# Moving the two layer-norm steps on GpSimd past the rotary products

## The reference

```python
x = L0_attn_x
x = x + attention(layernorm(x), qkv_w, proj_w, proj_b, slopes)
x = x + linear(layernorm(x), W, b, V_r, C)
# attention: q, k turned by rotary angles; softmax(q k^T * SCALE + alibi) v; projection
# linear:    x @ W.T + b + (x @ V_r) @ C.T
```

## Time and profile before

| | |
|---|---|
| median of 3 runs | 2132.45 us (2125.33 to 2133.05) |
| the profiled execution | 2133.05 us, of it span 2131.4 us |
| busy, share of the span | PE 98%, PEld 56%, DVE 89%, ACT 71%, POOL 61% |
| mean granted TensorE clock | 0.981 of full |
| one batch, 16 slots, in the steady part | 62.93 us |

### The profile page before, as it was taken

One profiled execution on the slowest core, in us unless ns is written; L12 is line 12 of the kernel. 1 busy time (PEld: TensorE's weight loads), 2 busy tenths in 40 slices (PEclk: granted clock), 3 DMA queues, 4 the chain that ended last, 5 costly groups with the idle time before them and its releaser, 6 DMA issues.

```text
span 2131.4 us, 81879 instructions
## 1 busy us (share of the span) xinstructions
PE 2080.3 (98%) x33572; PEld 1197.8 (56%) x33572; DVE 1894.1 (89%) x5439; ACT 1514.1 (71%) x2562; POOL 1301.3 (61%) x1095
## 2 busy tenths in 40 slices
PE   5999999999999999999999999999999999999996
PEld 2355555555555555555555555555555555555553
DVE  5699999999999999999999999999999999999972
ACT  2277777777777777777777777777777777777663
POOL 6356656666666667665666666666756566666512
PEclk8699999999999999999999999999999999999997
DMA  6233333333333333333333333333333333333301
GB/s 165 80 92 93 112 106 102 112 117 92 105 117 93 113 114 103 93 112 108 99 112 116 101 100 116 93 113 114 103 93 112 107 101 112 119 92 104 107 26 34
DMA packets 158887, 218.76 MB, mean 103 GB/s; under 512 B 19025, under 2 KB 104913, under 8 KB 158513
## 3 DMA queue, kind: packets, MB, share of 16 engines
q1 hardware_dynamic: 157232, 211.44, 33.4%
q10 hardware_dynamic: 1280, 2.10, 0.3%
HBM read 36.52 MB, written 16.78 MB: 25 GB/s over the span
## 4 chain that ended last, share of the span: by engine, by line
PE 91%; DVE 1%; issue 1%; ACT 1%; SPq 0%; POOL 0%; DMA 0%; DVEq 0%
PE ps_s L420 29%; PE ps_o L441 21%; PE ps_misc L404 18%; PE ps_misc L391 12%; PE ps_misc L378 3%; PE ps_misc L460 3%; PE ps_t L428 3%; PE ps_misc L451 2%; DVE junk L597 1%; ACT pt L783 0%; DVE x_hat L583 0%; ACT x_hat L731 0%; DVE ps_t L607 0%; ACT x_hat L726 0%; PE ps_s L404 0%
## 5 line engine op out<-in xcount | busy, mean ns | idle before, releaser
L597 DVE CUSTOM_DVE_ANT_0 junk<-ps_s,alibi 128x512 bf16<-128x512 f32 x2048 | 1332.0, 688 | 176.7 <-PE ps_s L420 135.8
L783 ACT ACTIVATE pt<-ps_t 128x1024 f32<-128x1024 f32 x1024 | 1049.8, 1026 | 462.5 <-DVE ps_t L607 448.3
L420 PE MATMUL ps_s<-at 64*128 64x512 f32 x2048 | 790.7, 462 | 12.8 <-DMA at<-halves 6.5
L428 PE MATMUL ps_t<-at 64*128 64x512 f32 x2048 | 759.6, 450 | 2.2 <-ACT pt L783 2.1
L441 PE MATMUL ps_o<-pt,v_one 128*17 128x128 f32 x16384 | 637.5, 273 | 1.4 <-ACT pt L783 1.4
L441 PEld LDWEIGHTS ps_o<-pt,v_one 128*17 128x17 f32 x16384 | 441.3, 98 | 184.2 <-issue 45.9
L607 DVE SCALAR_TENSOR_TENSOR ps_t<-diag,slope,ps_t 128x256 f32<-128x256 f32 x1024 | 489.6, 478 | 13.8 <-PE ps_t L428 13.8
L420 PEld LDWEIGHTS ps_s<-at 64*128 64x128 f32 x2048 | 337.1, 186 | 265.4 <-DVE row_max L597 150.1
L933 POOL TENSOR_TENSOR rope_b<-raw,rope_sin 128x512 f32<-128x512 f32 x128 | 164.8, 1287 | 340.4 <-ACT raw L763 340.3
L950 POOL TENSOR_TENSOR halves<-rope_a,swapped 128x512 fp32r<-128x512 f32 x128 | 161.7, 1285 | 314.7 <-DMA swapped<-rope_b 314.7
L428 PEld LDWEIGHTS ps_t<-at 64*128 64x128 f32 x2048 | 328.1, 184 | 15.6 <-ACT pt L783 10.9
(11 more groups left out here) (91 smaller groups left out, 1644.4 us busy)
## 6 DMA issues: line engine op xcount, KB each, us to landing
at<-halves SPq DMA_DIRECT2D x192, 512.0 KB, 3.7
swapped<-rope_b SPq DMA_DIRECT2D x256, 128.0 KB, 2.6
x_in<-in_L_attn_x_dram SPq DMA_DIRECT2D x32, 512.0 KB, 5.2
num<-o_sb SPq DMA_DIRECT2D x512, 32.0 KB, 2.0
x_res<-in_L_attn_x_dram SPq DMA_DIRECT2D x32, 512.0 KB, 5.3
out_dram<-x_hat SPq DMA_DIRECT2D x32, 512.0 KB, 6.0
at<-spread_den SPq DMA_DIRECT2D x60, 64.0 KB
at<-max_t ACTq DMA_DIRECT2D x128, 16.0 KB
```

What stands on the lines that cost most here:

```text
L420: pe.matmul(ps_s[:, t % 2, :], operand(n, 0)[:, t * P:(t + 1) * P], operand(n, 1), start=True, stop=True).then_inc(s_done, 1)
L428: pe.matmul(ps_t[:, j, :], operand(n, 1)[:, j * P:(j + 1) * P], operand(n, 0), start=True, stop=True).then_inc(t_done, 1)
L597: dve.tensor_tensor_reduce(junk[:, t % 2, :], ps_s[:, t % 2, :], alibi[:, off:off + N], 1.0, LOWEST, ALU.add, ALU.max, row_max[:, hb % 2, ...
L783: act.activation(pt[:, h % 2, 2 * pair:2 * pair + 2, :], ps_t[:, 2 * pair:2 * pair + 2, :], ACT.Exp).then_inc(exp_done, 1)
```

## The change

In POOL's loop, for every batch from 2 on, `deviation1` and `centre1` move from the head of slot 0 (after `split_max`, ahead of `normalise1`) to slot 15, behind the rotary products of that slot. `normalise1` stays in slot 0, behind `split_max`. `normalise2` stays in slot 5, but goes from ahead of the rotary products to behind them. Batches 0 and 1 keep their first layer norm as it was. No other engine's program changes.

```diff
                 b = batch_at(slot, -16)
                 if b and b > 1:
-                    deviation1(b)
-                    centre1(b)
                     normalise1(b)
-                b = batch_at(slot, 37)
-                if b is not None:
-                    normalise2(b)
                 cc = chunk_rotated(slot)
                 if cc is not None:
...
-                if sooner_at(slot, -17) == 1:
-                    deviation1(1)
-                    centre1(1)
+                b = sooner_at(slot, -17)
+                if b:
+                    deviation1(b)
+                    centre1(b)
                 if slot == -4:
                     normalise1(1)
+                b = batch_at(slot, 37)
+                if b is not None:
+                    normalise2(b)
```

## The result

The changed kernel takes 2228.52 us (median of 4 runs, 2222.86 to 2229.88) against 2128.89 us before (4 runs). The ratio is 1.0464, with an interval of 1.0431 to 1.0496: 4.6% slower, where 3.6% was forecast. The time lies 2.5 us above the top of the range. The profiled execution has a span of 2227.2 us, 95.8 more than before; the sum had said 76.3.

What follows compares the result with a forecast made beforehand. PE, busy 98% of the span, was taken as the bound. Its stalls, 30 x (2.03 - 0.24) = 53.7 plus 29 x 0.78 = 22.6, added 76.3 us to 2133.05: 2209 us, 3.6% slower, range 2184 to 2226.

Steps and rivals of the forecast that it cites:

- the sum: Whole kernel: 53.7 us from slot 0 and 22.6 from slot 5 make 76.3 us, giving 2209 us.
- Part 1: Slot 0: `split_max` ends later, PE's L451 2.03 us late, 0.24 given back; 30 times, 53.7 us net.
- Part 2: Slot 5: `normalise2` behind the products reaches PE 0.78 us late, 29 times, 22.6 us, nothing given back.
- The small doubt about the copy to `raw`: Before slot 7's products: PE's 0.24 us idle might go in 29 batches; at most 7 us faster, if stalls are absorbed.
- The clock falls: PE drops to 1.2 GHz after 2 us stalls: 66 us more, 2275; every other batch, 2242; chance 0.06.
- sign of being wrong: On PE: stalls followed by slices of lower clock would show the prediction wrong; the clock was to stay at 1.00.
- other rule that was weighed: On PE: weight loads busy only 36.60 of 62.95 us would leave room for 2.8 us per batch; loss could be nothing.
- Absorbed: DVE paces the kernel and PE's stalls fall in its room: not slower, 2133 or 2126 us; chance 0.05.
- one stall only: Slot 0 or 5: one stall does not come, 2156 or 2187 us; chance 0.12, shared with much given back.

## Why the prediction was off

A measure without start and tail: the time from the copy to `raw` ahead of the first moved `split_max` to the last copy to `raw`, one trace of each kernel. It is 1885.05 us before (109.84 to 1994.89) and 1981.92 in the changed kernel (108.18 to 2090.10).

| kernel | steady part, us above before | falls in it |
|---|---|---|
| changed | 96.9 | 13 |
| changed, stall filled | 76.9 | 1 |
| changed, L441 first | 65.7 | 1 |
| first layer norm only | 57.5 | 2 |
| the same, stall filled | 53.7 | 1 |
| second layer norm only | 21.8 | 0 |
| all three steps ahead | 159.4 | 30 |
| half of `centre1` | 31.1 | 1 |
| `deviation1` only | 0.4 | 0 |

**Part 1, right in place and size.** 2.03 us late and 0.24 given back were forecast, 1.79 net; the first move alone made a batch 64.72 us long in place of 62.93, 1.79 more. `split_max` was to end 6.96 us after the copy to `raw` began (1056.17 less 1049.21); it ended 6.95 after.

**Part 2, right.** 0.78 forecast, 0.76 measured. The order on POOL and the distance kept in slot 8 are as worked out. POOL waits 4.85 us for the copy to `raw` and not 3.6, but with the second move alone 3.69 us; so the other 1.2 us come with the stall of slot 0, and they cost nobody anything. The small doubt about the copy to `raw` is settled: no gain is to be had there.

**The sum of stalls, right.** 76.3 us; with PE kept at work the changed kernel is 76.7 us slower than before by the medians and 76.9 in the steady part of the trace.

**The rival "The clock falls" was what failed.** It was given 0.06 and left out of the range, as if it came whole or not at all, at 33 to 66 us on top. It came on top of the forecast: 13 falls of 30 at 1.6 us, 20 us, against the 2.2 us I had priced one at. It was also named as a sign of being wrong, and that sign came. The step that failed is the term at which the falling clock stood in the sum, nothing, and what put it there, the comparison with the earlier trace rows: I set a stall of 2 us beside one stretch with 1.78 us of work in 3.4 that stood at 1.00, found it nearer to that than to 4.5 us of nothing, and took one row as proof that such a gap is safe. The trace of before held a row that spoke against it, from the start of the kernel:

```profile
13.80:17.19 3.39, 1.63 (x11) 0.88 (x9) 3.25 (x5) 1.14 (x2) 0.76 (x1) 1.00 0.28 50
17.19:24.02 6.83, 3.67 (x36) 1.41 (x37) 6.83 (x36) 0.72 (x3) 0.00 (x0) 0.50 0.98 183
```

Here the clock fell at 17.19 behind a stretch in which PE had worked 1.63 of 3.39 us and had stood idle no longer than 0.69 us at a time. That is hardly less work than in the row that I took as proof, and so that row could not bear a price of nothing.

The experiments give this kernel's scale. In the steady batches there is no fall at stalls of 0.75, 1.13 and 1.43 us, at 2.00 us there are 12 of 29 in one kernel and 1 of 29 in another, and at 3.94 us all 29. The first stall of each of these kernels stands at the end of the start and is longer: at 1.91 us and more it brought a fall each time, at 0.80 none. The kernel before has no row with a gap of 2 us in a full stretch. What such a gap does was unknown, and an unknown cost has to go into the sum with both ends: from no fall to 30 of them, which by my own price would have taken the range to the 2275 of the rival.

The Trainium skill (TensorE: Matmul & The Clock Gate, HAM oscillation) warns of a gap in each tile after which the clock falls each time; its own case has gaps of some 3 to 5 us. The traces agree, with 3.94 us in every batch, and show that at 2.00 us, below the gaps of that case, it happens some of the time. The Trainium skill's other rule that was weighed (Perfetto Trace Analysis, Identifying the Most-Contended Engine), by which 58% of load time would have left PE room, is not borne out here: with the same load time in each batch, PE made up only 0.24 of 2.03 us.

**The other rivals.** Absorbed and one stall only are ruled out by 30 and 29 waits and by the two single moves. That PE is the one that cannot catch up is shown from its side by the swap of L441: 0.55 us of work in front of the wait made a batch 0.45 us shorter.

**Open.** Of the 29 stalls of 2.00 us in the changed kernel, the same to hundredths of a microsecond, 12 bring the clock down and 17 don't, and in the kernel with the first move alone it is 1 of 29. The even distances of 133.1 or 198.0 us between the falls speak against chance and for the moment at which a stall comes; what sets that moment was not tested. Whether the number of falls changes from run to run with one program isn't shown either, since one run of each kernel was traced.

## What to carry to other kernels

An engine at 61% with a strictly ordered list can still set the time: look up, for each result, how long it lies ready before the engine in front asks, and treat that slack (here 1.31 and 3.41 us) as the whole allowance for anything put ahead of it. Below it a move is free, above it costs nearly its full length if the waiting engine is the bound. If that engine is TensorE, a stall that repeats can have a second price, the lower clock behind it, here from 2 us on; put it in the sum with a bound, and if the wait can't go, put work in front of it that is due anyway.

## What the runs showed of the hardware

- A stall of PE of 2.00 us can be enough for the granted clock to go from 2.4 to 1.2 GHz. In the changed kernel it went down 1.0 to 1.6 us after PE had resumed, when it was already busy again; with the first move alone, once, 0.18 us before PE resumed. It costs 1.6 us each time here. At 3.94 us it happened each time, at 1.43 us and below in no steady batch.
- Two products whose result is thrown away, put into each stall but the first, made the kernel 20 us faster.
- In the steady batches a pass of GpSimd over 128x1024 took 1.89 us before and after, wherever it stood. At the start of the kernel one took 2.22 us; why, was not tested.
